# A residual whose bias comes by transfer: fill with the bias, then add x by an accumulating transfer

## What is computed

```
xn  = layernorm(x)                                   # x: 8192 rows of 512
a   = windowed attention of xn (16 heads, windows of 64 rows, relative bias)
out = x + (a @ proj_w + proj_b) + experts(xn)        # 8 experts, 1024 rows each
```

## Time and profile before

| | us |
|---|---|
| median of three runs | 2078.15 |
| lowest, highest | 2074.2, 2079.4 |
| the profiled execution | 2073.18 |
| its span, first to last instruction | 2071.4 |
| TensorE busy | 2002.7 |
| VectorE busy | 1164.5 |
| ScalarE busy | 662.7 |
| GpSimd busy | 593.7 |

### The profile page before, as it was taken

The page is one execution under the profiler, slowest core; times in us unless marked ns, Lnnn a source line. Parts: engine busy times, 40 slices in busy tenths (PEclk is TensorE's granted clock), DMA queues, the critical chain, the costliest instruction groups (busy, mean ns, idle before and its releaser), DMA issues.

```text
span 2071.4 us, 36039 instructions
## 1 busy us (share of the span) xinstructions
PE 2002.7 (97%) x15051; PEld 1621.8 (78%) x15051; DVE 1164.5 (56%) x1748; ACT 662.7 (32%) x1015; POOL 593.7 (29%) x368
## 2 busy tenths in 40 slices
PE   6999999999999999987899999999999999999997
PEld 5777877777878787765688888888888888888886
DVE  6666677778768777567644534345344543444221
ACT  3333333323244443322333233233332332324221
POOL 2444444444444443433122021211212012102111
PEclk9999999999999999988899999999999999999999
DMA  7222254445422222002444353233532434325311
GB/s 229 84 95 93 84 145 144 127 140 151 143 85 62 62 62 62 28 36 82 153 102 107 87 128 93 54 112 82 131 83 61 130 81 95 98 71 142 61 21 21
DMA packets 152882, 198.16 MB, mean 96 GB/s; under 512 B 19376, under 2 KB 93488, under 8 KB 152752
## 3 DMA queue, kind: packets, MB, share of 16 engines
q1 hardware_dynamic: 138416, 162.77, 26.1%
q0 software_dynamic: 14336, 33.56, 9.1%
HBM read 128.13 MB, written 51.38 MB: 87 GB/s over the span
## 4 chain that ended last, share of the span: by engine, by line
PE 51%; DVE 0%; POOL 0%; ACT 0%; issue 0%; POOLq 0%
PE ps_e L59 17%; PE ps_e L61 17%; PE ps_e L60 17%; PE ps_e L157 1%; POOL out_rows L1631 0%; DVE xn L1784 0%; DVE xgt_lo L1789 0%; ACT x_res L1699 0%; DVE w_lo L1778 0%; POOLq L1630 0%
## 5 line engine op out<-in xcount | busy, mean ns | idle before, releaser
L59 PE MATMUL ps_e<-xgt_hi,w_hi 128*128 128x512 f32 x1024 | 404.7, 395 | 7.7 <-DVE xgt_lo L1789 7.7
L60 PE MATMUL ps_e<-xgt_lo,w_hi 128*128 128x512 f32 x1024 | 399.4, 390 | 0.0
L61 PE MATMUL ps_e<-xgt_hi,w_lo 128*128 128x512 f32 x1024 | 399.3, 390 | 0.0
L1810 DVE TENSOR_TENSOR hm<-ps_e,silu 128x512 f32<-128x512 f32 x128 | 88.5, 691 | 462.6 <-PE ps_e L61 461.9
L59 PEld LDWEIGHTS ps_e<-xgt_hi,w_hi 128*128 128x128 f32 x1024 | 192.8, 188 | 46.0 <-DVE xgt_lo L1789 8.1
L503 POOL TENSOR_TENSOR pn_sb<-p_sb,s_rec 128x1024 f32<-128x1024 f32 x64 | 122.2, 1909 | 360.4 <-DVE s_rec L1169 291.9
L61 PEld LDWEIGHTS ps_e<-xgt_hi,w_lo 128*128 128x128 f32 x1024 | 192.7, 188 | 40.7
L1631 POOL DMA_INDIRECT out_rows<-x_res,idx x64 | 100.6, 1572 | 430.8 <-ACT x_res L1699 416.4
L60 PEld LDWEIGHTS ps_e<-xgt_lo,w_hi 128*128 128x128 f32 x1024 | 193.1, 189 | 38.0
L186 POOL DMA_INDIRECT x_in<-xn_rows,idx x64 | 76.1, 1190 | 486.2 <-DVE idx L178 308.7
L59 PE MATMUL ps<-xt_hi,wqk_hi 128*128 128x512 f32 x512 | 212.8, 416 | 0.0
(11 more groups left out here) (182 smaller groups left out, 3556.1 us busy)
## 6 DMA issues: line engine op xcount, KB each, us to landing
x_f<-in_w SPq DMA_DIRECT2D x48, 512.0 KB
raw<-in_w SPq DMA_DIRECT2D x48, 512.0 KB
x_res<-in_x SPq DMA_DIRECT2D x16, 1024.0 KB, 5.3
out_rows<-x_res SPq DMA_DIRECT2D x16, 1024.0 KB, 4.2
xn<-x_in SPq DMA_DIRECT2D x256, 64.0 KB, 2.0
xn_rows<-xt_plain SPq DMA_DIRECT2D x10, 1024.0 KB, 4.2
xn<-xn_rows SPq DMA_DIRECT2D x32, 256.0 KB, 5.1
x_in<-xn_rows SPq DMA_DIRECT2D x28, 256.0 KB, 4.6
```

The source lines that it names most:

```text
L59: nc.tensor.matmul(out, w_hi, x_hi, start=start, stop=False)
L60: nc.tensor.matmul(out, w_hi, x_lo, start=False, stop=False)
L61: return nc.tensor.matmul(out, w_lo, x_hi, start=False, stop=stop)
L1810: v.tensor_tensor(hm[:, m % 2, :], ps[:, 2 * (m % 2) + 1, :], silu[:, m % 2, :], ALU.mult).then_inc(hm_ready, 1)
```

## The change

SP fills x_res with the bias, read four times from its 256 KB in HBM, in the place of the load of x. GpSimd, at the place where it added the bias, issues a transfer that adds x from HBM onto x_res. VectorE waits for that transfer's semaphore, which counts 16 for each. The buffer p_bias and its load at the start are gone, so the constants' semaphore is waited for at 80.

```
             for u, (src, _, _) in enumerate(units):
                 if u == 2:
                     for dst, const in ((rel[:, :, :], d["rel"]), (qk_bias[:, :], d["qkb"]),
-                                       (v_bias[:, :], d["vb"]), (p_bias[:, :], d["pb"]),
+                                       (v_bias[:, :], d["vb"]),
                                        (same[:, :], d["same"]), (earlier[:, :], d["earlier"])):
...
             def load_res(c):
-                sp.dma_start(x_res[:, :, :], d["x"][c]).then_inc(res_loaded, 16)
+                sp.dma_start(x_res[:, :, :], d["pb"].unsqueeze(1).to_broadcast([P, TT, C])).then_inc(res_loaded, 16)
...
             def residual(c):

                 pool.wait_ge(res_loaded, 16 * (c + 1))
-                nc.gpsimd.tensor_tensor(x_res[:, :, :], x_res[:, :, :],
-                                        p_bias[:, :].unsqueeze(1).to_broadcast([P, TT, C]), ALU.add).then_inc(res_ready, 1)
+                pool.nop(nofuse=True)
+                nc.gpsimd.dma_start(out=x_res[:, :, :], in_=d["x"][c], accum_op=ALU.add).then_inc(res_ready, 16)
...
             def finish_rows(c, t, banks=P_BANK):
                 if t == 0:
-                    dve.wait_ge(res_ready, c + 1)
+                    dve.wait_ge(res_ready, 16 * (c + 1))
```

More of the change, by code:

```diff
@@ L220, in attention_block @@
         rel = sb("rel", [P, H, W])
-        v_bias, p_bias = sb("v_bias", [P, C]), sb("p_bias", [P, C])
+        v_bias = sb("v_bias", [P, C])
         ident, x_in, x_res, x_f = lists.ident, lists.x_in, lists.x_res, lists.x_f
@@ L531, in chunk @@
                 if not first and not hunting:
-                    pool.wait_ge(const_in, 96)
+                    pool.wait_ge(const_in, 80)
                     residual(c - 1)
@@ L730, in _ @@
                 split_hi(u)
-            act.wait_ge(const_in, 96)
+            act.wait_ge(const_in, 80)
             nc.scalar.activation(q_bias[:, :], qk_bias[:, 0:G], ACT.Copy, scale=SCALE).then_inc(q_bias_ready, 1)
@@ L1527, in _ @@
                 split_lo(u)
-            dve.wait_ge(const_in, 96)
+            dve.wait_ge(const_in, 80)
             dve.wait_ge(consts, 14)
```

## The result

| | before | after |
|---|---|---|
| median of 6 runs on the same chip, us | 2076.26 | 2086.32 |
| lowest, highest | 2074.2, 2081.99 | 2083.05, 2087.47 |
| span of the profiled execution | 2071.4 | 2084.1 |

What follows compares the result with a forecast made beforehand. TensorE, busy for 97% of the span, was taken as the bound. 2073.2 + 9.0 (regular chunks) - 4.3 - 2.7 (two late gains) = 2075.2, put against the median as 2080; range 2068 to 2106.

Steps and rivals of the forecast that it cites:

- the likeliest case: Result about the sum, with the accumulate's engine time from 5 to 6.4 us, within 0.3% of no change; chance 0.38.
- The fill: SP's bias transfer into x_res, in place of the load of x, hidden by 20 us of cover: costs nothing.
- The engine time A: Time for which 1 MB of accumulating transfer fills the 16 DMA engines: 5.9 us, between 3.6 and 8.2.
- the room: In a regular chunk VectorE can be 2.95 us late before TensorE stops at the gate matmuls.
- GpSimd's issue: GpSimd's own time to issue the accumulating transfer: 3 us, ends 1.6 and 6.5.
- the rival of the slow issue: Issue takes 6.5 us, x_res lands 1.9 us late in nine chunks: 2086.8, against the median 2092; chance 0.12.
- Packet by packet, all done by the end of the sum: Accumulate and bring-back transfers share the DMA engines in regular chunks, all done by 214.6 + A = 220.5 us.
- 1.0 us late per chunk, nine times: 9.0: TensorE stops before the gate matmuls in nine regular chunks alike: loss 9.0 us, bounds 0 and 30.
- The first place: One-hot multiply at 893.63, stretched to 5.01 us by the add; TensorE's wait until 900.43 shortens: gain 4.3 us.
- The second place: Attention's end, multiply at 972.15 stretched by the add; gain 2.7 us of 4.35 as x_res lands at 982.2.
- The cover: Rival: A below 4.9 or good overlap, no regular chunk loses, both gains full: 2064.5, against the median 2069.5; chance 0.25.
- The engines do fill up: Rival: A up to 8.2, gate matmuls 3.3 us late in nine chunks: 2098.2, against the median 2103; chance 0.25.

Runs made afterwards that it cites:

- e1: Kernel before with only the load of x replaced by the bias fill; GpSimd's add stays, x left out of the result: 2079.99 us, ratio 1.0004.
- e2: Changed kernel with the accumulating transfer of chunks 1 to 9 issued one softmax earlier: 2068.39 us, ratio 0.9958 to the kernel before.
- e3: Changed kernel with a plain transfer of the same bytes from GpSimd's queue in place of the accumulating one, bias left out: 2064.94 us, ratio 0.9936.
- e5: Kernel before, complete, with only the two GpSimd adds that lie across line 136 moved: 2068.49 us, ratio 0.9945.
- e8: Kernel before for the first nine residuals, fill and accumulating transfer from the tenth on, complete: 2066.28 us, ratio 0.9933.
- e6: Changed kernel with only tiles 0 and 1 of x accumulated, x left out of the other two: 2064.95 us, ratio 0.9923.
- e7: Changed kernel with GpSimd holding the accumulating transfer until the first of the four bring-back transfers has landed: 2110.82 us, ratio 1.0147.

## Why the prediction was right, and where it was off

The mechanism, the place and the order of the two effects were as forecast; the likeliest case gave a result of about no change, and the measured one is 10 us slower, inside the range but beyond what the prediction counts as no change. The range, 2068 to 2106, was wide, and that the result lies in it says less than the steps do:

*The fill: nothing.* It held (e1), with a doubt about the head.

*The engine time A, taken as 5.9.* It measures 6.3 to 6.8. A transfer that runs alone, at 625 us in chunk 10, where before the DMA engines are idle:

```profile
625.00:632.00 7.00, 7.00 (x53) 5.71 (x55) 3.21 (x6) 2.33 (x4) 1.90 (x1) 1.00 0.96 152
```

That is 6.7 us. Over the whole trace, GpSimd's queue fills 13.9% of 2084.1 us instead of 9.1% of 2071.4, so 6.3 for each of the 16; in e2 it is 14.4% of 2062.0, so 6.8. This term was mis-sized, and it weighs more than its size: the room was used up from 4.9 on, so 0.4 more is 40% more lateness. By the prediction's formula A = 6.3 gives 1.4 us late for each chunk, and 1.4 is how late the rows are in the chunk at 214 us, where TensorE stopped for 1.08. The rule that the prediction quotes from the Trainium skill's page Collectives: The Full Stack, twice the reads of a copy, gave 6.9 and a forecast of about 2090. The page has it for the reduce step of a collective, and its carrying over to this transfer was a guess; the trace agrees within some per cent, 6.3 over e3's 3.4 from the same queue, 1.85 times. Of the times named ahead its 2090 came nearest.

*GpSimd's issue, taken as 3.* It takes 1.33 us, and the rival of the slow issue is out. Issue, start and receipt together, taken as 4.7, are 2.7: the transfer issued alone at 623.41 lands 9.4 us later, with 6.7 of data. "Lands 12 to 14 us after its issue" held in five of the nine chunks (12.0 to 12.7); the other four have 9.7 to 11.9. The median of 10.0 is low because the last seven have little or nothing beside them. So x_res was in time in the chunk at 214 us (217.4 by the old clock, against 218.9) and past the room in three others, as shown above.

*Packet by packet, all done by the end of the sum.* It held in the chunk shown: 220.9, and the formula gives 220.5 with A = 5.9 and 220.9 with 6.3; 12.9 us from first issue to last landing against 12.6. Over the nine chunks it is 11.7 to 14.4, 13.5 in the mean.

*1.0 us late per chunk, nine times: 9.0.* Nine chunks did stop, each before the gate matmuls, for 1.6 us in the mean and not 1.0. The step that failed is "one chunk as the next". The four chunks like the one that the prediction worked out stop for 1.1 us in the mean, close to its 1.0; the five in which line 398's load is on the engines too stop for 2.0, and the prediction's count of what else is on them did not have that load. The sum also left out what a stop does next. Three of the nine, all among these five, are followed by 3.4 us at half clock, 5.1 us in all; the term for that was zero. And 1.9 us more stood at other waits. In place of 9.0 it is 22.1.

*The first place, gain 4.3.* It held to the tenth (4.32).

*The second place, gain 2.7.* The step that charged the late x_res failed. TensorE's gap shrank by the full 4.34, and the late landing costs nothing there (e5, e8). Around both places TensorE had a higher granted clock, 3.4 us that the sum did not have. In place of 7.0 it is 12.1.

Put together: 2073.2 + 0.1 + 3.2 + 22.1 - 0.2 - 12.1 = 2086.3, by the table above, against 2085.9 for the profiled execution. Terms of the forecast were small by 13 on the side of loss and by 5 on the side of gain, and that the two partly cancel is luck; the head's 3.2 is the part I can't assign.

*The rivals.* The cover does not hold for the accumulate, but it does for a plain transfer of the same bytes (e3) and for half of it (e6). The engines do fill up, at A = 6.3 to 6.8 and not 8.2; from 6.4 on the prediction had called the change slower by more than 0.3%, and it lies at that edge.

## What to carry to other kernels

A transfer that runs far from the path can still delay a small, urgent one that is issued just behind it: look at what is issued within its whole time on the engines, in every repeat and not in one, and move it (here one softmax earlier, 18 us). When a bound is a room that is used up, cost the overrun and not the transfer, and add to each stop of a full TensorE what the granted clock does after it. And before work is taken off an engine for good, see whether it hurts in one or two places only: moving two adds got the whole gain.

## What was not expected of the hardware

- 1 MB accumulated from HBM into SBUF from GpSimd's queue takes 1.33 us to issue, 6.3 to 6.8 us of the 16 engines, and 9.5 to 10.0 us to land in the median (up to 12.7 in after and 13.5 in e7, beside others). A plain transfer of the same bytes from the same queue takes 0.80 us to issue, 3.4 us of the engines, and lands after 6.2. It also goes out in 272 packets, the accumulate in 528 (the page's packet counts less those of before, over 16).
- Beside 2 KB packets, a stream of 512 B packets gets one packet for one, 43 KB in a microsecond instead of 250. In two chunks its first packet came only 4.3 us after its issue, where 1.0 is usual.
- SP's own issues are held up in it: in the chunk at 214 us the fourth of the four bring-back issues took 3.97 us, where the longest there was 0.49 before.
- A stop of 2.05 to 2.50 us of a TensorE that was otherwise full was followed by 3.4 us at half clock; after stops of 0.86 to 1.87 us none followed in after. In e7 the clock fell seven times between 92 and 590 us.
